# A Mamba-style scan block with a routed feed-forward on one core: ScalarE seeds two PSUM accumulators, injections go in pairs, and the instruction orders are rewritten

## The reference, cut to what matters

```python
uo = layernorm(x) @ W_in.T                    # u and o, 256 hidden channels each
u  = silu(causal_conv(u, 4 taps) + conv_b)
g  = u @ W_gate.T                             # delta_lo (64), b (16), c (16)
delta = softplus(delta_lo @ W_delta.T + delta_bias)
h_t = exp(A * delta_t) * h_(t-1) + (delta_t * u_t) * b_t      # 256 channels x 16 states
y_t = sum over states(h_t * c_t) + D * u_t
x1 = x + (y * silu(o)) @ W_out.T
n2 = layernorm(x1)
combine = top-2 softmax weights of n2 @ gate_w.T over 8 experts, normalised, * 2.5
out = x1 + sum_e combine_e * (silu(n2 @ wg_e) * (n2 @ wu_e)) @ wd_e  + shared expert(n2)
```

## Time and profile before

| | us |
|---|---|
| median of 3 runs | 1169.36 (1168.85 to 1170.06) |
| the profiled execution's own time | 1170.17 |
| its span, first to last instruction | 1168.5 |
| DVE, ACT, POOL, PE busy in the span | 1063.1, 1081.4, 1067.8, 1090.4 |
| first table load of line 638 (step k=2) | 103.96 |
| the 30th (step k=31) | 1086.65 |
| routing on DVE, from its first operation to the next `gated_up` (586.70 to 588.05) | 1.35 |
| length of one step in the middle (line 638 at 578.00, then at 611.78) | 33.78 |

### The profile page before, as it was taken

One profiled execution on the slowest core, in us unless ns is written; L12 is line 12 of the kernel. 1 busy time (PEld: TensorE's weight loads), 2 busy tenths in 40 slices (PEclk: granted clock), 3 DMA queues, 4 the chain that ended last, 5 costly groups with the idle time before them and its releaser, 6 DMA issues.

```text
span 1168.5 us, 25617 instructions
## 1 busy us (share of the span) xinstructions
PE 1090.4 (93%) x9075; PEld 925.3 (79%) x9075; DVE 1063.1 (91%) x1702; ACT 1081.4 (93%) x2182; POOL 1067.8 (91%) x502
## 2 busy tenths in 40 slices
PE   5667999999999999999999999999999999998898
PEld 4435888888888888888888888888888888887687
DVE  5577999999999999999999999999999999998974
ACT  6888999999999999999999999999999999998763
POOL 3699999999999999999999999999999999999930
PEclk9677999999999999999999999999999999998999
DMA  6344444333444433344444334444433344443000
GB/s 173 109 114 110 115 101 102 94 84 107 115 115 101 115 90 88 92 115 114 118 103 101 87 87 111 115 115 102 102 98 85 101 114 115 99 106 99 9 5 10
DMA packets 71481, 115.05 MB, mean 98 GB/s; under 512 B 8173, under 2 KB 30394, under 8 KB 71354
## 3 DMA queue, kind: packets, MB, share of 16 engines
q1 hardware_dynamic: 71354, 113.42, 37.7%
HBM read 41.04 MB, written 5.24 MB: 40 GB/s over the span
## 4 chain that ended last, share of the span: by engine, by line
ACT 60%; issue 14%; POOL 9%; DVE 9%; PE 6%; DMA 1%; ACTq 0%; DVEq 0%; POOLq 0%
ACT decay_ps L538 26%; ACT g_silu L525 5%; DVE decay_ps L758 5%; POOL inject L440 5%; POOL read L454 4%; ACT L655 3%; ACT L642 3%; ACT L638 3%; ACT L692 3%; ACT L668 3%; ACT xn L559 2%; ACT xn L567 2%; DVE features L780 2%; PE acc_ps L1174 2%; ACT L648 2%
## 5 line engine op out<-in xcount | busy, mean ns | idle before, releaser
L440 POOL TENSOR_TENSOR inject<-rep,bc 128x1024 f32<-128x1024 f32 x256 | 605.6, 2389 | 6.3 <-DMA rep<-dd 6.2
L454 POOL TENSOR_TENSOR read<-state,bc 128x1024 f32<-128x1024 f32 x192 | 456.7, 2388 | 29.1 <-DVE state L758 28.9
L758 DVE TENSOR_TENSOR_SCAN state<-decay_ps,inject 128x1024 f32<-128x1024 f32 x192 | 438.6, 2284 | 28.2 <-ACT decay_ps L538 27.3
L538 ACT ACTIVATE decay_ps<-rep,neg_a 128x255 f32<-128x255 f32 x1024 | 425.8, 463 | 2.9 <-DVE state L758 2.5
L1174 PE MATMUL acc_ps<-ffn_down,features 128*128 128x128 f32 (+1 forms) x1792 | 268.3, 279 | 0.4 <-DVE features L788 0.3
L1174 PEld LDWEIGHTS acc_ps<-ffn_down,features 128*128 128x128 f32 (+1 forms) x1792 | 235.1, 191 | 29.6 <-issue 24.9
L1137 PE MATMUL work_ps<-xn2T_part,ffn_gate 128*128 128x256 f32 x1344 | 213.5, 295 | 3.0 <-DVE dd L838 0.7
L1146 PE MATMUL work_ps<-xn2T_part,ffn_up 128*128 128x256 f32 x1344 | 206.7, 293 | 10.1 <-ACT g_silu L525 8.6
L1137 PEld LDWEIGHTS work_ps<-xn2T_part,ffn_gate 128*128 128x128 f32 x1344 | 175.7, 191 | 33.7 <-DVE dd L838 16.5
L1146 PEld LDWEIGHTS work_ps<-xn2T_part,ffn_up 128*128 128x128 f32 x1344 | 172.6, 189 | 33.5 <-ACT xnT_part L579 14.4
L780 DVE TENSOR_TENSOR features<-g_silu,work_ps 128x512 f32<-128x512 f32 x224 | 153.4, 686 | 11.2 <-PE work_ps L1146 10.7
(11 more groups left out here) (143 smaller groups left out, 1316.0 us busy)
## 6 DMA issues: line engine op xcount, KB each, us to landing
rep<-dd SPq DMA_DIRECT2D x256, 256.0 KB, 4.7
bc<-bc_rows SPq DMA_DIRECT2D x64, 512.0 KB, 4.0
x_in<-in_L_attn_x_dram SPq DMA_DIRECT2D x32, 128.0 KB, 2.2
out_dram<-result SPq DMA_DIRECT2D x32, 128.0 KB, 1.8
bc_rows<-g_sb SPq DMA_DIRECT2D x32, 32.0 KB
state<-in_L_ffn_w_gate_dram SPq DMA_DIRECT2D x1, 704.0 KB, 4.3
inject<-in_L_ffn_w_up_dram SPq DMA_DIRECT2D x1, 704.0 KB, 6.0
ffn_down<-in_L_ffn_w_down_dram SPq DMA_DIRECT2D x1, 704.0 KB, 7.5
```

Source lines behind the costliest of these rows:

```text
L440: pool.tensor_tensor(inject[:, slot:slot + many], du_all, b_all, ALU.mult).then_inc(inject_done, many)
L454: pool.tensor_tensor(read[:, slot:slot + many], state[:, first:first + many], c_all, ALU.mult).then_inc(read_done, many)
L538: last = act.activation(decay_ps[:, at % 2, j, 1:T], rep[(HALVES * n + half) % RP][:, j, 0, 1:T], ACT.Exp, scale=neg_a[:, col:col + 1])
L758: dve.tensor_tensor_scan(to, decays, inject[:, at % RI].rearrange("p j t -> p (j t)"), 0.0, ALU.mult, ALU.add).then_inc(state_done, 1)
```

## The change

1. **Seeds.** `skip_term` and its matrix are gone. ACT's new `seed_skip(n, half)` writes D times u into `y_ps`, and the sums add onto it; it waits for `take_y` of the half before. ACT's new `seed_x1(n)` writes x1 into `down_ps`, and `down` adds onto it. `add_result` on DVE is replaced by `copy_result` on ACT. PE waits on the new semaphores `y_seeded` and `down_seeded`. Four identity matmuls go ahead of everything on PE.
2. **Pairs.** Injections are made two groups at a time (128x2048), 4 in a step in place of 8, with RI=6 buffers in place of 4. The reads stay single.
3. **Transposes.** `turn_xn` and `turn_xn2` use the transpose mode.
4. **Statistics.** One `bn_stats` over both tiles, read interleaved, replaces two `bn_stats` and two `bn_aggr`; the function fills its even and odd halves with the two tiles' moments.
5. **Orders.** The bodies of all engines are written anew, with other banks. ACT changes tables 5 times a step: silu, exp, softplus, silu, exp. PE no longer starts `ups 0`, `gates 0`, `gates 1` at the same places; `down 7` and up, for the sequence before, move later. SP stores the result after `spread_delta`.
6. **Start.** ACT loads the exp/ln table before anything else and keeps it through the first layernorm; the two diagonal matrices of D are no longer made.

```diff
-STAGED, LOADED = 2, 5
+STAGED, LOADED = 4, 5
-RX, RU, RI, RS, RR, RP = 5, 3, 4, 3, 3, 3
+RX, RU, RI, RS, RR, RP = 5, 3, 6, 3, 3, 3
-GATE_BANK = [2, 0, 0, 1, 0, 1, 2]
-UP_BANK = [1, 2, 0, 1, 0, 0, 2]
-COMB_BANK = [1, 1, 0, 2, 0, 2]
+GATE_BANK = [0, 2, 0, 2, 0, 0, 2]
+UP_BANK = [1, 1, 0, 1, 1, 1, 2]
+COMB_BANK = [0, 2, 0, 2, 2, 0]
...
+            def seed_skip(n, half):
+                act.wait_ge(u_done, n + 1)
+                act.wait_ge(y_taken, HALVES * n + half)
+                act.activation(y_ps, u[n % RU][:, half, :], ACT.Identity,
+                               scale=skip_d[:, half:half + 1]).then_inc(y_seeded, 1)
+            def seed_x1(n):
+                act.wait_ge(x1_done, n + 1)
+                act.wait_ge(result_done, n)
...
+                act.copy(down_ps, x1[n % 2][:].rearrange("p j d -> p (j d)")).then_inc(down_seeded, 1)
+            def copy_result(n):
+                act.wait_ge(down_mm, CHUNKS * (n + 1))
+                act.wait_ge(stored[n % 2], 16 * (n // 2))
+                act.copy(result[n % 2][:].rearrange("p j d -> p (j d)"), down_ps).then_inc(result_done, 1)
...
-                dve.wait_ge(ln1_var, TILES * n)
-                for j in range(TILES):
-                    last = dve.bn_stats(stats1[:, j, :], x_in[n % RX][:, j, :])
-                last.then_inc(stats1_done, 1)
+                dve.bn_stats(stats[:, 0, :], x_in[n % RX][:].rearrange("p j d -> p d j")).then_inc(ln1_var, 1)
...
-                                     skip_group_check=True)
+                                     is_transpose=True, skip_group_check=True)
```

More of the change, by code:

```diff
@@ L649, in body @@
                 if on(-2):
+                    silu(k - 2, 0)
+                if later(2):
+                    norm1(k + 2)
+                if on(-2):
+                    silu(k - 2, 1)
                     silu(k - 2, 2)
                     silu(k - 2, 3)
+                if on(0):
+                    seed_skip(k, 0)
                 if on(1):
@@ L910, in body @@
                     scan(k, 1)
-                if on(1):
-                    dve.wait_ge(gate_done, k + 2)
-                if on(-2) and not on(1):
-                    dve.wait_ge(h_done, PAIRS * (k - 2) + 2)
+                if k == 0:
+                    stats_x(3)
+                if on(-2):
+                    dve.wait_ge(silu_done, PAIRS * (k - 2) + 4)
+                if on(-2) and not on(-2):
+                    dve.wait_ge(silu_done, PAIRS * (k - 2) + 2)
                 if on(-2):
                     route(k - 2)
-                    gated_up(k - 2, 2)
+                if on(-1):
+                    add_x1(k - 1)
+                if on(-2):
                     comb_low(k - 2)
-                if on(-3):
-                    add_result(k - 3)
                 if on(0):
@@ L923, in body @@
                 if on(-1):
-                    add_x1(k - 1)
                     stats_x1(k - 1)
-                if later(3):
-                    moments_x(k + 3)
                 if on(-2):
+                    gated_up(k - 2, 2)
                     gated_up(k - 2, 3)
@@ L957, in body @@
                 if on(0):
-                    scan(k, 6)
+                    scan(k, 7)
+                if on(-1):
+                    shift_logits(k - 1)
+                if later(4) and k != -1:
+                    stats_x(k + 4)
                 if on(-2):
                     weigh(k - 2, 4)
-                if on(-1):
-                    shift_logits(k - 1)
-                if on(0):
-                    scan(k, 7)
+                    weigh(k - 2, 5)
+            dve.wait_ge(prep, PARTS + 2)
             stats_x(0)
-            moments_x(0)
             dve.wait_ge(conv_loaded, 16 * len(conv_loads))
@@ L991, in _ @@
                               ALU.subtract).then_inc(weights_ready, 1)
-            for half in range(HALVES):
-                dve.tensor_scalar(skip[:, half, :], ident[:], skip_d[:, half:half + 1], None,
-                                  ALU.mult).then_inc(weights_ready, 1)
             dve.wait_ge(prep_a, 1)
@@ L1084, in project_z @@
                 last.then_inc(z_mm, 1)
-            def skip_term(n, half):
-                pe.matmul(y_ps, skip[:, half, :], u[n % RU][:, half, :], start=True, stop=False, skip_group_check=True)
             def sum_states(n, q):
@@ L1319, in body @@
                 if on(-1):
-                    gates(k - 1, 0)
+                    logits(k - 1)
+                    pe.wait_ge(xn2T_low, k)
+                    ups(k - 1, 0)
+                    pe.wait_ge(shifted_done, k)
+                if on(-2):
+                    spread_comb(k - 2, 5)
+                    down(k - 2, 6)
                 if on(0):
                     sum_states(k, 5)
-                if on(-2):
-                    down(k - 2, 7)
-                    pe.wait_ge(hc_done, COMBS * (k - 2) + 5)
-                if on(-1):
-                    gates(k - 1, 1)
+            pe.wait_ge(consts, 1)
+            for j in range(4):
+                pe.matmul(acc_ps[:, j * P:(j + 1) * P], ident[:], ident[:], start=(j == 0), stop=(j == 3),
+                          skip_group_check=True)
             turn_conv()
```

301 lines of the change are left out of this document (134 added, 167 removed).

## The result

The changed kernel takes 1157.57 us (median of 4 runs, 1157.48 to 1158.41) against 1169.71 for the kernel before, run beside it: ratio 0.9899 [0.9882, 0.9916]. That is 12.1 us faster. The forecast was 1147, so 22.7 of gain; the direction holds, the size is about half. The measured time lies inside the range of 1125 to 1163 and outside the 1141 to 1152 that the forecast gave itself.

What follows compares the result with a forecast made beforehand. It took no one engine as the bound, but a loop ACT, DVE, ACT with POOL close behind. 1170.2 - 20 (29 steps) - 1 - 1.5 = 1147.7, with the median 0.8 below the profiled execution: 1147; range 1125 to 1163.

Steps and rivals of the forecast that it cites:

- ACT's term: ACT work per step: two table loads go (-2.60 us), four activations come (1.34), net -1.2, to 31.7.
- POOL's term: POOL work per step: four pairs of injections at 4.5 us each give -0.7, to 32.3.
- rival B: POOL sets the step, at 33.3 to 33.4 us with its wait for rep: 1155 us, chance 0.17.
- DVE's term: DVE work per step: result add and paired statistics go, two wider statistics come, net about -0.85 us, to 31.7.
- PE's term: PE work per step: skip term -0.86 us, transposes -0.43, together -1.3.
- The walk of one step: One step followed in the new order by distances between starts, from scan 0: 33.1 us against 33.8, -0.7.
- points 1 and 5: DVE from scan 0 to scan 1, gated_up 1 done at 4.8 us; and ACT's decays 1 at the step's end.
- Point 5: End of the step on ACT: next step's decays 1 start at 31.2 behind scan 7, end at 32.8, in time.
- Rival C: A new wait at seed_skip 0 eats the gain if sum 7 comes 0.7 later: 1167 to 1171 us, chance 0.12.
- Rival A: The stalls go too, only POOL's 32.3 to 32.5 is left: -1.4 a step, 1127 us, chance 0.10.
- Rival D: PE's clock falls after idle gaps of some 2 us in every step: +3.1 a step, 1260 us, chance 0.07.
- Start and end: Outside the steady steps: first two steps -1 us, start -1.5 (0 to -3), last three steps 0, 3 either way.

Runs made afterwards that it cites:

- a_loads: The changed kernel with two table loads more (exp, and silu again) between silu 1 and silu 2: 1198.58 us.
- a_single: The changed kernel with each pair of injections split into two single ones at the same place, 6 buffers kept: 1160.55 us.
- t_dve: The changed kernel with weigh 4 and 5 over half their columns, DVE work left out only to see what moves: 1156.76 us.
- b_transpose: The kernel before with the one-pass transposes alone: 1168.86 us, ratio 0.9993.
- b_seeds: The kernel before with both seeds and the result copy on ACT, no skip term on PE, no result add on DVE, seven table loads: 1208.04 us.
- a_no_transpose: The changed kernel with its two transposes as fp32 matmuls again: 1167.01 us.
- t_both: The changed kernel with down 9 and 12 made for one tile and weigh 4 and 5 over half their columns: 1156.30 us.

## Why the prediction was right, and where it was short

*ACT's term* holds. Five table loads a step; busy -1.15 where -1.2 was said. From a load's start to the next activation's it is 1.30 again (578.75 to 580.05), and two more loads cost 2.58 in `a_loads` (594.39 to 596.97). The Trainium skill's drain of about 1380 ns (page "ScalarE: Activation LUTs", "What ACT_TABLE_LOAD costs") isn't seen after the change either: by the page's figures two loads would be 5.3, an estimate. `seed_skip` takes 0.48 by its length and 0.42 to the next start (0.40 said), the seed of x1 and the copy 0.38.

*POOL's term* holds. The pair has a mean of 4.57 in ten steps (4.5 said from start to start, and 4.52 is seen there), busy -0.72 where -0.7 was said:

```profile
L438 POOL TENSOR_TENSOR inject<-rep,bc 128x2048 f32<-128x2048 f32 x40 | 183.0, 4574 | 6.8 <-DMA rep<-dd 6.8
```

The Trainium skill's 4497 ns for such an operation (GPSIMD Engine Reference, 3.1) agrees with the 4574 here to within 2%. But the term was worth little: `a_single` takes it away and the step stays. POOL isn't the bound, so rival B is out, though its number, 1155, is nearer to the result than the forecast is; that is chance.

*DVE's term* was too large: -0.52 of busy time where -0.85 was said. The statistics of two interleaved tiles take 0.41 to 0.42 (0.35 said; bounds 0.25 and 0.49). It would have decided nothing: `t_dve` cuts 0.41 more (320.76 to 316.69 in ten steps) and gives 0.8 us in all.

*PE's term* was the worst sized: -0.22 of busy time where -1.3 was said. `b_transpose` shows -0.29 for the transposes alone (327.79 of PE in its ten steps against 330.73 in the earlier trace rows), where 0.43 was said. The skip term's 0.86 is hardly seen: `b_seeds`, which has lost it too, has 32.7 of PE a step (314.67 / 338 x 35.11), 0.4 less than before. The busy time of rows that overlap isn't the sum of their lengths, and groups behind a wait are longer (below). PE now also waits 0.22 a step for a seed and 0.25 for `xn2_high`. It doesn't have the slack of 1.3 that was counted on: `a_no_transpose` adds 0.26 of step for what was to be hidden.

*The walk of one step is what failed*, in its points 1 and 5. It has `gated_up 1` done at 4.8 after scan 0; the trace has 5.10 (576.96 - 571.86). Two distances account for most of it: scan 0 to `gated_up 0` is 2.29 where 2.18 was taken, because `gated_up 0` waits for silu 0 (below), and `read_own 0` to the clear is 1.28 where 1.13 was taken, because the clear waits for the read's end. On PE, gates 2 start at 2.32, behind silu 0 and sum 6, and the three groups up to sum 7 take 2.34 where three times 0.71 was taken; so `take_y` starts at 5.36 (5.1 said) and the seed at 5.88 (5.5). The gate, the load and decays 2 follow on a full ACT, so scan 2 starts at 9.89 (9.55 said), `times_u` ends at 17.2 (16.7), scan 5 starts at 24.00 (23.5), and the next scan 0 at 33.36 (33.0). The shift arises in the first 6 us of the step, and nothing behind it gives it back. From k=2 to k=31 it makes the steps give 11.0 where 20 was said.

*Point 5* said that ACT's decays 1 of the next step end "in time", and the walk stopped there. But the router's exponentials, a load and silu 0 come behind them, and both `gated_up 0` and gates 2 need silu 0. In three steps of the changed kernel silu 0 ends at 574.07, 607.44 and 640.84, and `gated_up 0` starts at 574.15, 607.53 and 640.93: ACT's loop is closed in the changed kernel itself. DVE's wait there is only the 0.1 by which 2.29 exceeds 2.18, too little for a row of the waits; `t_dve` and `t_both` make it 0.45, and the step doesn't move. So the gain of 1.15 on ACT went as far as 0.35 to 0.40 into the step; the rest became idle time of ACT, 33.38 - 31.72 = 1.66 a step, of which 1.23 is the wait ahead of silu 3 and 0.1 the one ahead of the seed. The kernel before had 0.9 of idle time, most of it ahead of silus too: its ACT waited 5.3 for gates and 1.3 for `gated_up` in ten steps.

*Rival C* (a new wait eats the gain) was right in kind and in place, and wrong in size: the chain through sum 7, `take_y` and `seed_skip 0` was named, and the walk had `take_y`'s wait (0.3; 0.27 measured). But that chain was to have "0.05 to spare"; it brought scan 2 0.34 late, and C priced a delay of 0.7 only. Rival A is out: the stall of `times_u` behind a load is there (0.26). Rival D is out: the granted clock is 1.00 in the ten steps.

*Start and end.* Up to k=2 the change gives -0.8 where start and first steps were to give -2.5; from k=31 on it gives nothing, as said. 9 us in the steps and 1.7 at the start make the 10.7 by which the profiled execution (1158.41) missed the 1147.7 of the sum.

*Which part earned it?* Alone on the kernel before, transposes and statistics give 0, the pairs cost 17 and the seeds cost 38. Together, with the new orders and two loads fewer, they give -12. So no part is worth a number of its own. What seems to pay is that the new order needs two loads less: `a_loads` puts two loads back at another place and loses 41. How much belongs to the order and how much to the loads isn't separated. Not tried, and so left open: sum 7 ahead of gates 3 on PE, which would let `take_y` and the seed go sooner. By the distances above it could give 0.2 a step at most, an estimate; then silu 3, behind `gated_up 1`, holds the seed. A third `g_silu` buffer alone would lift the wait of 1.23 and leave the seed where it is, since `take_y` holds it.

*The signs of being wrong* were four prices: statistics over 0.6, pairs over 4.7, ACT's writes over 0.5, gaps of PE over 1 us ahead of sum 7. None came true (0.42, 4.57, 0.48, none), and the step was still 33.4 and not 33.1. They watched the parts, and what was wrong was the loop.

## What to carry to other kernels

When every engine is 95% to 98% busy, walk each loop that returns to itself, not only the engines' sums: here one loop set the step, another two came within some 0.2 us of it, and cutting PE's work, DVE's or both beside it gave nothing. The largest new wait is the first place to look at after a change, but not always the one that counts: here it was 1.23 us ahead of silu 3, and what released ACT last was one instruction later, behind an idle time of 0.09 that no view lists. Follow what each start waited for by its time, instruction by instruction, until you are back at the first. A walk needs the error of its distances beside it: 0.3 us in 33 is half of a gain of 0.7.

## What the runs showed of the hardware

- A group of matmuls that had just been released took about 0.1 us longer, where the trace shows no idle PE. Down 7 and 8, released by the seed, take 1.00 for their eight records (578.27 to 579.27), eight in a run 0.92 (601.39 to 602.31). Gates 2 take 0.81 to the next start (574.18 to 574.99) and ups 1 behind them 0.72, the 0.71 of the earlier trace rows. A release isn't the only thing that costs this: gates 3 take 0.81 too (575.71 to 576.52), though silu 1, for which they wait, had ended at 575.3. The waits list an idle 0.4 of the weight loads at about a dozen places a step.
- ACT wrote into the bank that PE then adds onto as fast as elsewhere: 478 ns on average for 128x256 with a scale, in twenty of them, against 464 for a decay activation of 128x255.
- One POOL operation of 2048 elements saves little over two of 1024: 4.52 from start to start against 2 x 2.36, so 0.2.
- From `times_u` to the injection that needs it, via the transfer, took 9.3 in this step (622.43 to 631.72) where 8.0 was taken. It cost POOL 1.82 of idle time, and the reads behind it came late for the sums, so that gates 2 started 0.7 behind silu 0: the step that began at 638.93 lasted 33.99 in place of 33.38. The chain that ended last goes by this transfer and the reads (last rows below). In the ten steps before it the way took 7.9 to 8.3 and POOL waited 0.4 to 0.9; one of these steps was long too (33.73, behind the 0.9), the others took 33.35 to 33.40.

```profile
621.74 0.69 DVE L829 TENSOR_TENSOR dd<-work_ps,u 128x512 f32<-128x512 f32 x1 [0.26 <-ACT dd L615]
```

```profile
631.72 4.55 POOL L438 TENSOR_TENSOR inject<-rep,bc 128x2048 f32<-128x2048 f32 x1 [1.82 <-DMA rep<-dd]
```

```profile
625.01 6.59 DMA rep<-dd
...
638.55 2.39 POOL read L452
```
